# The first tap of a depthwise convolution made on ScalarE, one PSUM bank per channel group, the coefficients on their own semaphore

## What is computed

```python
def _mamba_fallback(h, W_in, conv_w, conv_b, W_out):           # D_INNER = 512, D_CONV = 4
    xz = einsum('btd,ed->bte', h, W_in)
    xp, z = split(xz, 2, axis=-1)
    xc = depthwise_causal_conv(xp, conv_w, 4 taps) + conv_b    # along t, each channel by itself
    y = silu(xc) * silu(z)
    return einsum('bte,de->btd', y, W_out)
h = _rmsnorm(x);  x = x + _mamba_fallback(h, W_in, conv_w, conv_b, W_out)
h = _rmsnorm(x);  m = einsum(relu(einsum(h, W_mlp1)), W_mlp2)
return x + m
# the caller: x = x + this stage(layernorm(x))
```

## Time and profile before

| | us |
|---|---|
| median of three executions | 679.4 |
| lowest, highest | 678.47, 685.2 |
| the profiled execution, as timed | 682.74 |
| its span, first to last instruction | 680.9 |
| convolution stage in it, from the first issue to that of the next stage | 563.3 to 604.1 |

### The profile page before, as it was taken

The page is one execution under the profiler, slowest core; times in us unless marked ns, Lnnn a source line. Parts: engine busy times, 40 slices in busy tenths (PEclk is TensorE's granted clock), DMA queues, the critical chain, the costliest instruction groups (busy, mean ns, idle before and its releaser), DMA issues. The chain is left out here.

```text
span 680.9 us, 12861 instructions
## 1 busy us (share of the span) xinstructions
PE 583.0 (86%) x4813; PEld 395.7 (58%) x4813; DVE 498.0 (73%) x852; ACT 396.1 (58%) x750; POOL 335.5 (49%) x265
## 2 busy tenths in 40 slices
PE   4976899997899999799953878878788988889997
PEld 3542355444677777587730555545455575668886
DVE  4357999996678885479966999999999945433322
ACT  4226975552435554456775999999899943421111
POOL 1009999996204442244605898998878830000000
PEclk9987999999999999999975898897887769999999
DMA  9526600000927664046547788897859638900000
GB/s 354 237 74 252 247 0 1 0 1 0 310 83 238 212 210 140 17 127 176 149 130 161 147 141 172 156 175 155 162 132 159 122 64 337 398 1 1 0 1 15
DMA packets 97090, 92.90 MB, mean 136 GB/s; under 512 B 70595, under 2 KB 88323, under 8 KB 93638
## 3 DMA queue, kind: packets, MB, share of 16 engines
q1 hardware_dynamic: 93760, 90.46, 47.9%
q10 hardware_dynamic: 3270, 1.65, 0.8%
HBM read 68.59 MB, written 6.62 MB: 110 GB/s over the span
## 5 line engine op out<-in xcount | busy, mean ns | idle before, releaser
L2150 DVE TENSOR_REDUCE d_nmax<-d_psum 128x1 f32<-128x1024 f32 x128 | 151.5, 1212 | 5.2 <-PE d_psum L2306 5.2
L2306 PE MATMUL d_psum<-kst,qT 96*128 96x512 bf16 x256 | 90.7, 452 | 38.2 <-ACT d_e L2247 15.7
L528 POOL TENSOR_TENSOR b_h<-b_h,b_cb 128x1024 f32<-128x1024 f32 x32 | 88.2, 2756 | 6.3 <-DVE b_h L578 4.5
L2247 ACT ACTIVATE d_e<-d_psum,d_nmax 128x1024 f32<-128x1024 f32 x64 | 71.3, 1115 | 14.9 <-DVE d_nmax L2150 14.4
L2130 POOL TENSOR_SCALAR d_rounded<-d_e,d_lift 128x1024 f16<-128x1024 f32 x64 | 72.1, 1127 | 13.8 <-issue 6.8
L2130 POOL TENSOR_SCALAR d_rounded<-spare,d_lift 128x1024 f16<-128x1024 f32 x62 | 70.4, 1135 | 16.0 <-ACT d_lift L2251 11.8
L578 DVE TENSOR_TENSOR_SCAN b_h<-b_dA,b_psum 128x1024 f32<-128x1024 f32 x32 | 73.1, 2285 | 2.5 <-ACT b_dA L633 2.0
L633 ACT ACTIVATE b_dA<-b_dtT,b_A 128x248 f32<-128x248 f32 x128 | 53.7, 490 | 33.1 <-DVE b_h L578 28.1
L2247 ACT ACTIVATE spare<-d_psum,d_nmax 128x1024 f32<-128x1024 f32 x64 | 71.4, 1122 | 1.9 <-DVE d_nmax L2150 1.9
L689 PE MATMUL b_psum<-b_bdiag,b_dtx 128*128 128x512 f32 x128 | 60.2, 594 | 0.8 <-DVE b_h L578 0.8
L2333 PEld LDWEIGHTS d_psum<-d_ident_f,d_rounded 128*128 128x128 f16 x512 | 40.8, 115 | 32.5 <-issue 18.9
(11 more groups left out here) (439 smaller groups left out, 1189.3 us busy)
## 6 DMA issues: line engine op xcount, KB each, us to landing
c_w<-in_w0gu SPq DMA_DIRECT2D x16, 768.0 KB, 4.8
kst<-kT_scratch SPq DMA_DIRECT2D x84, 128.0 KB, 2.7
w<-in_w SPq DMA_DIRECT2D x5, 1920.0 KB, 21.3
b_cb<-c_scratch SPq DMA_DIRECT2D x4, 2048.0 KB, 7.1
c_w<-in_w0dn SPq DMA_DIRECT2D x16, 384.0 KB, 5.6
kT_scratch<-k_kT SPq DMA_DIRECT2D x12, 384.0 KB, 3.7
a_ctx<-in_ctx SPq DMA_DIRECT2D x2, 2048.0 KB, 18.8
k_ctxT<-in_ctxT SPq DMA_DIRECT2D x12, 256.0 KB, 3.1
```

Source lines behind the costliest of these rows:

```text
L528: nc.gpsimd.tensor_tensor(hv, hv, cv, ALU.mult).then_inc(hc_ready, 1)
L2150: nc.vector.tensor_reduce(nm[:, t, m:m + 1, f:f + 1], quarter(m, j).unsqueeze(1), AX.X, ALU.max, negate=True).then_inc(nm_ready, 1)
L2247: nc.scalar.activation(e[j].unsqueeze(1), quarter(m, j).unsqueeze(1), ACT.Exp, bias=nm[:, t, m:m + 1, f], accum_out=zp[:, t, m:m + 1, f]). ...
L2306: last = nc.tensor.matmul(quarter(m, j)[:, b * 512:(b + 1) * 512], qT[0:QROWS, m:m + 1, t * P:(t + 1) * P], kst[m % 2][0:QROWS, at:at + 51 ...
```

## The change

convolve(c) loses its first instruction. ScalarE gets a loop over the four groups ahead of its silus: for each it waits for the chunk and writes xc[:, c, :] = Identity(scale * x + bias), with scale and bias read from conv, one value a partition, and raises the new semaphore tap_ready, for which convolve(c) now waits. The x chunks go to banks 0 to 3, one each (x_psum), and the z chunks to banks 6 and 7 (z_psum), so that group c waits for c + 1 chunks and no longer for a pair. The load of conv gets its own semaphore conv_in, for which VectorE and ScalarE wait in place of weights_in; TensorE waits for the other three loads. The MLP keeps the old places under the name halves.

```diff
--- before.py
+++ after.py
@@ -2425,6 +2425,7 @@
         ps = banks("e_psum")
         ln = LayerNorm(nc, sb, sem, "e_ln")
         chain = sem("e_dve_chain")
+        conv_in = sem("e_conv_in")
         weights_in = sem("e_weights_in")
         y_ready = sem("e_y_ready")
         ss_ready = sem("e_ss_ready")
@@ -2433,6 +2434,7 @@
         hT_psum = sem("e_hT_psum")
         hT_ready = sem("e_hT_ready")
         xz_psum = sem("e_xz_psum")
+        tap_ready = sem("e_tap_ready")
         xc_ready = sem("e_xc_ready")
         sx_ready = sem("e_sx_ready")
         sz_ready = sem("e_sz_ready")
@@ -2442,13 +2444,20 @@
         mh_ready = sem("e_mh_ready")
         mlp_psum = sem("e_mlp_psum")
 
-        def xz(c):
+        def halves(c):
             return ps[:, c // 2, (c % 2) * T:(c % 2 + 1) * T]
+
+        def x_psum(c):
+            return ps[:, c, 0:T]
+
+        def z_psum(c):
+            return ps[:, 6 + c // 2, (c % 2) * T:(c % 2 + 1) * T]
 
         with nc.Block() as block:
             @block.sync
             def _(sp):
-                for dst, name in ((conv, "conv"), (w_out, "w_outT"), (mlp1, "mlp1T"), (mlp2, "mlp2T")):
+                sp.dma_start(conv[:], d["conv"]).then_inc(conv_in, 16)
+                for dst, name in ((w_out, "w_outT"), (mlp1, "mlp1T"), (mlp2, "mlp2T")):
                     sp.dma_start(dst[:], d[name]).then_inc(weights_in, 16)
                 for n in range(CHUNKS1 // LOAD1):
                     own = slice(n * LOAD1, (n + 1) * LOAD1)
@@ -2464,18 +2473,16 @@
                 step = Steps(dve, chain)
                 ln.vector(dve, step, y, x, each=y_ready)
                 rms_norm(nc, dve, step, hn, y, ss, root_ready, 1, hn_ready)
-                dve.wait_ge(weights_in, 64)
+                dve.wait_ge(conv_in, 16)
 
                 def gate(c):
                     dve.wait_ge(sx_ready, c + 1)
                     dve.wait_ge(sz_ready, c // 2 + 1)
                     nc.vector.tensor_tensor(gy[:, c, :], sx[:, c, :], sz[:, c, :], ALU.mult).then_inc(gy_ready, 1)
                 def convolve(c):
-                    dve.wait_ge(xz_psum, c // 2 * 2 + 2)
-                    step(nc.vector.tensor_scalar(xc[:, c, :], xz(c), conv[:, c, CONV - 1:CONV], conv[:, c, CONV:CONV + 1],
-                                                 ALU.mult, ALU.add))
+                    dve.wait_ge(tap_ready, c + 1)
                     acc = xc[:, c, :].rearrange("p (b l) -> p b l", l=L)
-                    src = xz(c).rearrange("p (b l) -> p b l", l=L)
+                    src = x_psum(c).rearrange("p (b l) -> p b l", l=L)
                     for j in range(1, CONV):
                         ins = nc.vector.scalar_tensor_tensor(acc[:, :, j:L], src[:, :, 0:L - j],
                                                              conv[:, c, CONV - 1 - j:CONV - j], acc[:, :, j:L],
@@ -2520,9 +2527,15 @@
                 root(y, 1)
                 copy_hT(hT, 1)
                 act.preload_act_table(ACT.Silu)
+                act.wait_ge(conv_in, 16)
+                for c in range(EC):
+                    act.wait_ge(xz_psum, c + 1)
+                    nc.scalar.activation(xc[:, c, :], x_psum(c), ACT.Identity, bias=conv[:, c, CONV:CONV + 1],
+                                         scale=conv[:, c, CONV - 1:CONV]).then_inc(tap_ready, 1)
+
                 def silu_z(c):
                     act.wait_ge(xz_psum, EC + 2 * c + 2)
-                    nc.scalar.activation(sz[:, 2 * c:2 * c + 2, :], ps[:, 2 + c, :].rearrange("p (c t) -> p c t", c=2),
+                    nc.scalar.activation(sz[:, 2 * c:2 * c + 2, :], ps[:, 6 + c, :].rearrange("p (c t) -> p c t", c=2),
                                          ACT.Silu).then_inc(sz_ready, 1)
 
                 def silu_x(c):
@@ -2555,11 +2568,11 @@
                 pe.wait_ge(g["w_inT_in"], 16)
                 for c in range(2 * EC):
                     for k in range(KC):
-                        last = nc.tensor.matmul(xz(c), w_in[:, k, c * P:(c + 1) * P], hT[:, k, :], start=(k == 0),
+                        last = nc.tensor.matmul(x_psum(c) if c < EC else z_psum(c - EC), w_in[:, k, c * P:(c + 1) * P], hT[:, k, :], start=(k == 0),
                                                 stop=(k == KC - 1))
                     last.then_inc(xz_psum, 1)
                 keep_warm(nc, g, ps[:, 5, :], 3)
-                pe.wait_ge(weights_in, 64)
+                pe.wait_ge(weights_in, 48)
                 for c in range(EC):
                     pe.wait_ge(gy_ready, c + 1)
                     for t in range(TC):
@@ -2573,7 +2586,7 @@
                 pe.wait_ge(hT_ready, 2)
                 for c in range(MC):
                     for k in range(KC):
-                        last = nc.tensor.matmul(xz(c), mlp1[:, k, c * P:(c + 1) * P], h2T[:, k, :], start=(k == 0),
+                        last = nc.tensor.matmul(halves(c), mlp1[:, k, c * P:(c + 1) * P], h2T[:, k, :], start=(k == 0),
                                                 stop=(k == KC - 1))
                     if c % 2:
                         last.then_inc(m_psum, 1)
```

## The result

The changed kernel is 0.4% faster. Over 20 executions of each its median is 679.07 us (674.79 to 682.05) against 682.53 us (677.49 to 686.23) before. The medians lie 3.5 us apart; the ratio estimated from all executions is 0.9956 with a 95% interval of 0.9936 to 0.9976, that is 3.0 us less, between 1.6 and 4.4. Of the three executions shown ahead of the prediction (median 679.4), two are among the five shortest of the 20 of before.

What follows compares the result with a forecast made beforehand. VectorE was taken to bound the convolution stretch from 572.94 us, its start set by mlp2's load; TensorE would bound it afterwards. TensorE's end moving from 584.29 to 581.2 gives 3.1 us, so 679.4 becomes 676.3, range 674.7 to 680.2.

Steps and rivals of the forecast that it cites:

- The sum: Convolution stage: TensorE's next fillers after w_out start at 581.2 instead of 584.29 us, a gain of 3.1 us.
- the term 16 x 0.22 = 3.52: w_out on TensorE: sixteen records of 0.22 us run without a pause from 577.64 to 581.2 us.
- the alternative pitch: w_out on TensorE: records at 0.215 us, the filler's pitch, instead of 0.22, for a gain of 3.2 us.
- The 0.38: TensorE's three fillers before w_out: 0.38 us taken as the part of a filler beyond its issue pitch.
- the 0.2 that TensorE was to keep from VectorE's gain: VectorE brings gate(1) forward 3.3 us; 0.2 goes uncollected, since TensorE isn't free for w_out's group 1 before 578.52.
- the base: Whole execution: the starting time of 679.4 us, median of the known executions, from which the gain was subtracted.
- a change that does nothing: Rival, chance 0.04: something read as moving is pinned elsewhere, such as a load; whole time stays 679.4 us.
- 679.6: Whole time in us that the profiled execution of 682.74 would take after the change.
- The own range of the gain: Whole kernel: gain of 2.7 us with a tap of 1.12 us, up to 3.3.
- The reload of the table: Definite form of the late-gates rival (0.09): ScalarE loads tables around the taps, 1.28 us each; gain 2.1, time 677.3.
- ScalarE as the bound: Rival, chance 0.03: taps delay silus and gates; gain gone at 1.8 us a tap, 680.9 us at 2.2.
- VectorE's adds were not slowed by ScalarE beside them: Answers a rival, chance 0.06: parallel PSUM reads slow both engines, convolutions stay at 1.97 us; gain 1.1, time 678.3.

Runs made afterwards that it cites:

- the run with two taps: Changed kernel with each tap on ScalarE made twice; stretch from the chunks' first matmul to the first add on y 11.63 us, against 11.31 in the changed kernel.
- the experiment: Changed kernel with each tap on ScalarE made four times and ten more TensorE fillers ahead of w_out; stretch 14.65 us, granted clock 1.00.
- taps four times: Changed kernel with each tap on ScalarE made four times, without added fillers; stretch 15.48 us, stage 41.73 us.

## Why the prediction was right or wrong

The mechanism of the gain held, step by step; what failed is the time from which it was counted. All times count from the first matmul of the chunks, which is 569.98 in the prediction and 572.36 in the profile of after:

| step | predicted | measured |
|---|---|---|
| duration of a tap | 0.57 | 0.56 |
| first tap starts | 1.25 | 1.26 |
| first add on VectorE | 1.86 | 1.94 |
| gate(0) | 6.14 | 6.18 |
| gate(1) | 7.86 | 7.91 |
| w_out starts | 7.66 | 7.65 |
| its next fillers start | 11.2 | 11.11 |
| gain of the stretch | 3.1 | 3.20 |

**The sum** was 0.1 short. 0.06 of it is the term 16 x 0.22 = 3.52: without a pause the sixteen records take 583.47 - 580.01 = 3.46, 0.216 each. The rest is rounding, since 584.29 - 577.64 - 3.52 is 3.13. The 0.22 came from the chunks' stream, and the prediction gave the alternative pitch and its 3.2. Two readings beside the sum were off. The 0.38 is the whole duration of a filler and not the part beyond its pitch (the pitch, 0.215, came out right all the same). And the 0.2 that TensorE was to keep from VectorE's gain is 0.03: the gate of group 1 was in time by 580.01 + 4 x 0.216 - 580.27 - 0.47 = 0.13 us, and the twelve records behind a pause would have taken 0.1 longer. The cap was at the right engine, and thinner than said.

**The step that failed is the base.** The prediction took its 3.1 us from 679.4, the median of three executions, to 676.3, and allowed 0.7 us for a median over other executions. Over 20 executions the kernel before has a median of 682.53, 3.1 above that of the three: over four times what was allowed, and as much as the whole gain. Seen from 682.53, the forecast of 676.3 is a change of 6.2 us, and the measured one is 3.0 (3.5 between the medians). The prediction had a sign of this in hand: of the four executions that it knew, the profiled one stood at 682.74 and another at 685.2. The profiles show where executions differ, mostly in the stage ahead of this one, by some 5 us. With such a spread the median of three needs no cause beyond chance to lie 3 us off, and none is shown.

That the measured 679.07 lies inside 674.7 to 680.2 is luck. It is 2.8 above the forecast and 0.3 below the 679.4 that the prediction gave for a change that does nothing, in the part that the range kept for less gain or none, though the gain was there in full. Luck too is the closeness of 679.6, named for the profiled execution: the profiled execution of after took 681.98, 2.4 more than that, with its convolution stage beginning 2.4 later.

**Within 1%** was right, with its chance of 0.95. That a per cent is about what can be told was too coarse for 20 executions, whose interval is 0.4% wide and doesn't reach a ratio of 1.

**The own range of the gain**, 2.7 to 3.3, held for the stretch (3.20). The whole gave 3.0 in one set of executions and 4.1 in the other, each with an interval of 2.8 us or more, so it neither bears the range out nor speaks against it. Its lower end, 2.7 for a tap of 1.12 us, has a neighbour in the run with two taps, 0.90 us a group, which gave 14.51 - 11.63 = 2.88.

**The rivals.** The reload of the table didn't happen: there is no ACT_TABLE_LOAD between L2529 and the silus. The Trainium skill (ScalarE: Activation LUTs, Table sets: the hidden batching unit) says that identity is in every set. The trace agrees for the Silu set. ScalarE as the bound needed 1.8 us a group and got 0.56; the experiment put the point where it was worked out, with the clock held. What that rival overlooked is that a late gate also leaves TensorE idle, and that 2.3 us of idleness cost another 0.83 in clock: its price above the point was too low. VectorE's adds were not slowed by ScalarE beside them: nine in 4.23 us, 0.47 each, as before. One instruction of the first tap takes 0.54 us on VectorE and 0.56 on ScalarE, and moving it was worth 1.65 us, because ScalarE was idle and VectorE the bound. The Trainium skill (ScalarE: Activation LUTs, Rules for kernel authors) puts multiplications and additions on VectorE. These rows agree on the single instruction, by 0.02 us; as advice for this stretch it did not hold.

## What to carry to other kernels

Work out for a stretch not only what leaves the engine that is the bound but when the next engine would be done by itself. Here the two came out 0.03 us apart, and past that point less work on VectorE (a third of its adds away) is worth nothing. A wait on a shared semaphore hides the value of whatever only lets the work behind it start earlier: the banks gave 0 behind the load and 0.86 without it. It doesn't hide what makes that work shorter: the tap on ScalarE gave 1.65 behind the same load. So take such waits away before you judge the first kind. And before a small gain is put on an absolute time, look at how far executions of one kernel lie apart: compare the stage and not the span, and don't take the base of an absolute time from three executions.

## What the runs showed of the hardware

- A pause of 2.30 us of TensorE was followed by a granted clock of 0.51 over two us and 0.64 over the next two, and by 1.00 in the two after that; it cost 0.83 us over sixteen records. Pauses of 1.59 and 1.10 us left it at 1.00.
- An activation of 128 x 256 float32 from PSUM to SBUF with scale and bias from one column each takes 0.56 us. Sixteen in a row start 0.45 us apart throughout, while the duration shown for one grows from 0.56 to 0.65 (taps four times).
- The same load of 1 MB of weights landed 2.49, 2.70 and 2.96 us after the first matmul in three profiles (the changed kernel with the old wait, the banks alone, and before); with a wait on it the stretch moved by just that.
